# An attention and FFN kernel: the FFN's matmuls dealt between the attention steps of later batches

## What is computed

```python
# x (8, 256, 512): 8 batches, 256 channels, 512 positions; mask (8, 512)
Q, K, V = (proj(W) for W in (Wq, Wk, Wv))          # 16 heads of 16 channels
att = softmax((Q @ K.T / 4 + b) * m + (1 - m) * -1e30)
y = att @ V                                        # back to (8, 256, 512)
gate, up = y @ Wg.T, y @ Wu.T                      # 512 -> 4096, weights of 4-bit codes x scales per 32
gelu = tanh(0.7978845608 * (gate + 0.044715 * gate**3)) * gate * 0.5 + gate * 0.5
out = x + (gelu * up) @ Wd.T                       # 4096 -> 512
```

## Time and profile before

| | us |
|---|---|
| median of 3 runs (lowest to highest) | 1612.29 (1604.95 to 1619.18) |
| the profiled execution | 1610.11 |
| its span, first to last instruction | 1608.3 |
| busy in the span: PE / DVE / ACT / POOL | 1510.4 / 695.6 / 534.6 / 270.4 |
| mean granted clock of PE | 0.937 |
| moved by DMA | 63.04 MB, mean 39 GB/s |

### The profile page before, as it was taken

One profiled execution on the slowest core, in us unless ns is written; L12 is line 12 of the kernel. 1 busy time (PEld: TensorE's weight loads), 2 busy tenths in 40 slices (PEclk: granted clock), 3 DMA queues, 4 the chain that ended last, 5 costly groups with the idle time before them and its releaser, 6 DMA issues.

```text
span 1608.3 us, 19482 instructions
## 1 busy us (share of the span) xinstructions
PE 1510.4 (94%) x7376; PEld 597.7 (37%) x7376; DVE 695.6 (43%) x1113; ACT 534.6 (33%) x701; POOL 270.4 (17%) x146
## 2 busy tenths in 40 slices
PE   3989889898989889999999999999999999999999
PEld 1222222222322224444444444444444444444444
DVE  5858676776777562323323233323233232122122
ACT  1447464564656463222222222222222222111111
POOL 2012112121211212122112212211221221000000
PEclk7779896897898899999999999999999999999999
DMA  5112221212221103001001000100100010000000
GB/s 165 44 51 59 65 63 43 61 44 57 67 69 42 51 21 124 20 20 40 20 20 33 26 20 20 39 20 20 36 23 20 20 39 1 0 26 26 0 26 26
DMA packets 32662, 63.04 MB, mean 39 GB/s; under 512 B 5584, under 2 KB 14928, under 8 KB 32480
## 3 DMA queue, kind: packets, MB, share of 16 engines
q1 hardware_dynamic: 29760, 59.42, 12.5%
q10 hardware_dynamic: 2848, 2.90, 0.5%
HBM read 49.43 MB, written 12.61 MB: 39 GB/s over the span
## 4 chain that ended last, share of the span: by engine, by line
PE 82%; DMA 6%; DVE 5%; SPq 3%; ACT 2%; issue 1%; ACTq 1%; POOL 1%; POOLq 0%; DVEq 0%
PE psum L828 14%; PE psum L830 14%; PE psum L829 14%; PE psum L769 7%; PE psum L899 7%; PE psum L901 7%; PE psum L900 7%; PE psum L798 6%; DMA wide<-seed_rows 4%; DVE maxima L638 3%; PE psum L784 3%; PE psum L756 2%; PE psum L805 1%; PE psum L746 1%; DMA wide<-max_lo 1%
## 5 line engine op out<-in xcount | busy, mean ns | idle before, releaser
L638 DVE TENSOR_REDUCE maxima<-psum 128x1 f32<-128x512 f32 x512 | 332.3, 685 | 161.9 <-PE psum L769 158.3
L703 DVE SCALAR_TENSOR_TENSOR small<-psum,small 128x512 f32<-128x512 f32 x128 | 88.5, 691 | 592.6 <-issue 306.6
L544 ACT ACTIVATE big<-psum 128x1024 f32<-128x1024 f32 x256 | 253.4, 1024 | 214.8 <-PE psum L784 198.2
L769 PE MATMUL psum<-wide 51*128 51x512 f16 x512 | 211.3, 447 | 68.3 <-DMA wide<-seed_rows 51.1
L580 ACT ACTIVATE small<-psum 128x512 f32<-128x512 f32 x128 | 76.4, 597 | 421.1 <-PE psum L830 421.1
L334 POOL TENSOR_TENSOR dq_w<-dq_code,dq_scales 128x1536 f32<-128x1536 f16 x32 | 109.8, 3433 | 541.8 <-DVE dq_code L371 541.8
L590 ACT CAST in_hi<-small 128x512 f16<-128x512 f32 x128 | 79.1, 618 | 361.8 <-DVE small L703 361.8
L828 PE MATMUL psum<-y_hi,wide 128*128 x512 | 194.1, 379 | 2.6 <-POOL wide L346 2.6
L828 PE MATMUL psum<-y_hi,w_even_hi 128*128 (+1 forms) x512 | 194.2, 379 | 1.2 <-POOL w_even_lo L346 1.2
L829 PE MATMUL psum<-y_lo,w_even_hi 128*128 (+1 forms) x512 | 194.0, 379 | 0.0
L830 PE MATMUL psum<-y_hi,w_even_lo 128*128 (+1 forms) x512 | 194.0, 379 | 0.0
(11 more groups left out here) (83 smaller groups left out, 1366.2 us busy)
## 6 DMA issues: line engine op xcount, KB each, us to landing
dq_packed<-packed SPq DMA_DIRECT2D x32, 384.0 KB
dq_scales<-scales SPq DMA_DIRECT2D x32, 384.0 KB
wide<-qk_parts SPq DMA_DIRECT2D x64, 128.0 KB
qk_parts<-wide SPq DMA_DIRECT2D x60, 128.0 KB
small<-x SPq DMA_DIRECT2D x8, 512.0 KB, 4.1
wide<-qk_parts SPq DMA_DIRECT2D x64, 64.0 KB
big<-x SPq DMA_DIRECT2D x4, 1024.0 KB, 9.5
out<-big SPq DMA_DIRECT2D x16, 256.0 KB, 2.1
```

Of the source, the lines that this page charges most:

```text
L544: nc.scalar.activation(p_exp[:, k, :, i], p_score[:, 2 * i:2 * i + 2, :], ACT.Exp, scale=SCORE_SCALE).then_inc(exp_done, 1)
L638: nc.vector.reduce_max(maxima[:, g % 2, n:n + 1], p_max[:, n % 2, :], AX.X).then_inc(max_red, 1)
L769: nc.tensor.matmul(p_max[:, n % 2, :], q_stack[rows, side, s, t * P:(t + 1) * P], k_stack[rows, side, s, :], start=True, stop=True).then_i ...
```

## The change

The FFN now goes by chunks of two batches, all 32 units for one chunk, and chunk c is worked on while attention computes batches 2c+2 and 2c+3. One generator, `schedule()`, gives all engines one order. Batches 0 and 1 (`SOLO`) and the first steps of batch 2 run alone. Then each attention step that PE takes part in is followed by `len(rest) // left` FFN steps of the chunk. An FFN step is three matmuls: `G0` to `G3` gate, `U0` to `U3` up, `D` one of 16 down steps, which come after each fourth unit for the four units before. Chunk 3 runs after attention is over.

- Weights are decoded in chunk 0 (two units ahead; the first two in batches 0 and 1), used from a ring of 8 units (`w_ring`), stored in DRAM as fp16 halves (`spill_unit`, 0.79 MB) and reloaded in the later chunks three units ahead (`reload_unit`).
- PSUM in the mixed part: one pair of banks for scores (before: two), gate bank 2, up bank 3, the sums in 2 and 3 too (before: gate and up two banks each, sums four). In chunk 3 gate and up alternate again.
- Max tiles of batches 2 on are made in pairs, upper and lower rows, and one `reduce_pair` reads both banks. PE issues nothing at an even `m` and two tiles at an odd one.
- Gelu becomes `square` (ACT), `cubic` (DVE), `tanh` (ACT), `gelu_part` (DVE), `inter_part` (DVE); the remainder of the result moves from DVE to POOL (`inter_low`). One `inter` buffer in place of two; five slots of `in_hi` and `in_lo`.
- DVE adds to `acc` after every 4 units: 128 additions in all, before 64. `acc` holds one chunk; rows are loaded and stored by chunk.
- Decode has no separate sign and magnitude tiles; packed codes and scales have two slots. The loops of the FFN are unrolled.

```diff
-GROUPS = 4
-UNITS = F // P // GROUPS
+UNITS = F // P
+GROUP = 4
+RING = 2 * GROUP
+AHEAD_UNITS = 2
+LAST_CHUNK = (CHUNKS - 1) * UNITS
+LAST_SHARED = LAST_CHUNK // GROUP - 1
+SOLO = 2
...
+        def gate_bank(u):
+            return psum[:, 0 if u > LAST_CHUNK and u % 2 else 2, :]
+        def up_bank(u):
+            return psum[:, 1 if u > LAST_CHUNK and u % 2 else 3, :]
+        def out_bank(j, r):
+            return psum[:, 2 + r % 2 if j < LAST_SHARED else 4 + r, :]
...
+        def ffn(c):
+            for u in range(UNITS * c, UNITS * (c + 1)):
+                for step in ("G0", "G1", "G2", "G3", "U0", "U1", "U2", "U3"):
+                    yield u, step, None
+                if u >= GROUP and u % GROUP == 0:
+                    for r in range(4):
+                        for i in range(GROUP):
+                            yield u, "D", (u // GROUP - 1, r, i)
+            if c == CHUNKS - 1:
+                for step in ("G0", "G1"):
+                    yield STEPS, step, None
+                for r in range(4):
+                    for i in range(GROUP):
+                        yield STEPS, "D", (STEPS // GROUP - 1, r, i)
...
+        def schedule():
+            steps = list(attention())
+            ready = [n + 1 for n, (b, g, step, _) in enumerate(steps) if step == "YN" and g == 0 and b >= 2 and b % 2 == 0]
+            for b, g, step, arg in steps[:ready[0]]:
+                yield "attention", b, g, step, arg
+            for c in range(CHUNKS):
+                rest = list(ffn(c))
+                span = steps[ready[c]:ready[c + 1]] if c < CHUNKS - 1 else []
+                left = sum(on_pe(step) for _, _, step, _ in span)
+                for b, g, step, arg in span:
+                    yield "attention", b, g, step, arg
+                    if on_pe(step):
+                        count = len(rest) // left
+                        left -= 1
+                        for u, name, part in rest[:count]:
+                            yield "ffn", u, None, name, part
+                        rest = rest[count:]
+                for u, name, part in rest:
+                    yield "ffn", u, None, name, part
...
@@ scalar
+            for kind, b, g, step, arg in schedule():
+                if kind == "ffn":
+                    u = b
+                    if step == "G0" and u:
+                        inter_high(u - 1)
+                    elif step == "G1" and u + AHEAD_UNITS < UNITS:
+                        weight_scale(act, u + AHEAD_UNITS)
+                    elif step == "G2" and SOLO <= u + AHEAD_UNITS - 1 < UNITS:
+                        weight_hi(act, u + AHEAD_UNITS - 1)
+                    elif step == "G3":
+                        square(u)
+                    elif step == "U1":
+                        tanh(u)
+                    continue
...
@@ gpsimd
+                    if step == "G1" and u:
+                        inter_low(u - 1)
+                    elif step == "G3" and SOLO <= u + AHEAD_UNITS - 1 < UNITS:
+                        weight_lo(pool, u + AHEAD_UNITS - 1)
+                    elif step == "U2" and u + AHEAD_UNITS < UNITS:
+                        weight_f(pool, u + AHEAD_UNITS)
...
@@ vector
+            def reduce_pair(b, g, n):
+                dve.wait_ge(max_mm, 16 * q + n + 2)
+                nc.vector.reduce_max(maxima[:, g % 2, n // 2:n // 2 + 9:8], p_max, AX.X).then_inc(max_red, 2)
...
+            def cubic(u):
+                dve.wait_ge(square_s, u + 1)
+                nc.vector.scalar_tensor_tensor(out=gelu[:, u % 2, :], in0=gelu[:, u % 2, :], scalar=1.0,
+                                               in1=gate_bank(u), op0=ALU.add, op1=ALU.mult).then_inc(cubic_s, 1)
+            def gelu_part(u):
+                dve.wait_ge(tanh_s, u + 1)
+                nc.vector.scalar_tensor_tensor(out=gelu[:, u % 2, :], in0=gelu[:, u % 2, :], scalar=1.0,
+                                               in1=gate_bank(u), op0=ALU.add, op1=ALU.mult).then_inc(gelu_s, 1)
...
+            for kind, b, g, step, arg in schedule():
+                if kind == "ffn":
+                    u, n = b, b + AHEAD_UNITS
+                    if step == "G1" and n < UNITS:
+                        decode(dve, n, 0)
+                    elif step == "G2" and n < UNITS:
+                        decode(dve, n, 1)
+                    elif step == "G3" and n < UNITS:
+                        decode(dve, n, 2)
+                    elif step == "U0":
+                        cubic(u)
+                    elif step == "U1" and n < UNITS:
+                        decode(dve, n, 3)
+                    elif step == "U2":
+                        gelu_part(u)
+                    elif step == "U3":
+                        inter_part(u)
+                    elif step == "D" and arg[2] == GROUP - 1:
+                        add_rows(arg[0], arg[1])
...
@@ tensor
-                wait_from(pe, max_red, 16 * (4 * b + g) + n - 1)
-                e, i, t = n // 8, n // 4 % 2, n % 4
+                if b_now < SOLO or n % 2 == 0:
+                    wait_from(pe, max_red, 16 * (4 * b + g) + n - (1 if b_now < SOLO else 0))
+                e, i, t = n % 2, n // 8, n // 2 % 4
...
-                wait_from(pe, exp_done, n - 1)
+                wait_from(pe, exp_done, n - 1 if b < SOLO else n)
+                bank = 2 * i if b < SOLO else 0
...
+            def wait_bank(u, used, freed):
+                if u > LAST_CHUNK:
+                    wait_from(pe, freed, u - 1)
+                elif u > GROUP and u % GROUP == 1:
+                    pe.wait_ge(acc_add, 4 * (u // GROUP - 1) + used + 3)
+                else:
+                    wait_from(pe, freed, u)
...
@@ sync
+                    if step == "G0" and u < STEPS:
+                        if u + AHEAD_UNITS + 1 < UNITS:
+                            load_unit(sp, u + AHEAD_UNITS + 1)
+                        if UNITS <= u + AHEAD_UNITS + 1 < STEPS:
+                            reload_unit(sp, u + AHEAD_UNITS + 1)
+                    elif step == "U2" and u + AHEAD_UNITS - 1 < UNITS:
+                        if u == 0:
+                            spill_unit(sp, 0)
+                        spill_unit(sp, u + AHEAD_UNITS - 1)
```

More of the change, by code:

```diff
@@ L104, in build @@
             "p (e k o) -> p e k o", e=2, k=CK)[:, e] for e in range(2)] for i in range(3)]
-        gelu = small[:, 0:1024].rearrange("p (i t) -> p i t", i=2)
-        inter = small[:, 1024:2048].rearrange("p (i t) -> p i t", i=2)
+        gelu = sb("gelu", [P, 2, T], f32)
+        inter = sb("inter", [P, T], f32)
         av_sb = sb("av_sb", [P, T], f32)
@@ L186, in build @@
         acc_in = sem("acc_in")
+        w_out = [sem(f"w_out{i}") for i in range(RING)]
+        w_in = [sem(f"w_in{i}") for i in range(RING)]
         gate_mm = sem("gate_mm")
         up_mm = sem("up_mm")
+        square_s = sem("square_s")
+        cubic_s = sem("cubic_s")
+        tanh_s = sem("tanh_s")
         gelu_s = sem("gelu_s")
@@ L256, in head_of, with attention, on_pe @@
             return 8 * (g // 2) + 4 * e + 2 * (g % 2) + i
-        def batches(eng, body):
+        def attention():
             for b in range(B):
-                body(b, b % 2, b == 0, b == B - 1)
+                yield b, 0, "any", None
+                for g in range(QUADS):
+                    for step, arg in plan(g, b == 0, b == B - 1):
+                        yield b, g, step, arg
+            for step in ("A2", "A3", "AO", "Y", "YN"):
+                yield B, 0, step, None
+        def ffn(c):
[12 more added lines that the diff above has]
+                        yield STEPS, "D", (STEPS // GROUP - 1, r, i)
+        def on_pe(step):
+            return step[0] in "SmAY" and step not in ("AO", "YN") or step == "MT" or step[0:2] in WORK and step[2] in "ab"
+        def schedule():
[17 more added lines that the diff above has]
+                    yield "ffn", u, None, name, part
         def wait_from(eng, sem, value):
@@ L267, in wait_from @@
                 eng.wait_ge(sem, value)
-        def chunks(eng, body):
-            for g in range(GROUPS):
-                if g == 0:
-                    body(0, 0)
-                with eng.Fori(1 if g == 0 else 0, CHUNKS) as t:
-                    body(g, t)
         def wait_apart(eng, spare, sem, value):
@@ L597, in _, with square, tanh @@
-            chunks(act, chunk)
+            def square(u):
+                act.wait_ge(gate_mm, u + 1)
+                wait_from(act, inter_s, u - 1)
+                nc.scalar.activation(gelu[:, u % 2, :], gate_bank(u), ACT.Square,
+                                     scale=GELU_A ** 0.5 / (Y_SCALE * W_SCALE)).then_inc(square_s, 1)
+            def tanh(u):
+                act.wait_ge(cubic_s, u + 1)
+                nc.scalar.activation(gelu[:, u % 2, :], gelu[:, u % 2, :], ACT.Tanh,
+                                     scale=GELU_B / (Y_SCALE * W_SCALE)).then_inc(tanh_s, 1)
@@ L820, in _ @@
             for n in range(AHEAD):
```

(19 more changed lines are left out.)

530 lines of the change are left out of this document (253 added, 277 removed).

## The result

The changed kernel takes 1656.14 us (median of 4 runs, 1652.05 to 1662.40), the kernel before 1614.82 in runs beside it: a ratio of 1.0268, 95% interval 1.0207 to 1.0329. The prediction was 1574 in 1530 to 1650: the sign was wrong and the time lies above the range. Its profiled execution took 1662.4 us, its span is 1660.6; the sum that was forecast for that span is 1572.5, so 88 us are to be found. The profiled execution is the slowest of the four, 6 us above the median.

A forecast was written before the change was run, and what follows sets the result against it. It took attention's PE idling and half clock as the bound, the FFN having nothing left to gain. Solo 179, mixed work 1071, waits 36 + 20, chunk 3 266.5 made a span of 1572.5; with 1.5 more, 1574 us, range 1530 to 1650.

The forecast's parts named there:

- Solo: Batches 0 and 1 up to the first YN of batch 2, running alone: forecast to end at 179 us.
- that YN: First YN step of batch 2, end of the solo part: claimed reached at 175.4 us in the old kernel.
- the head's loads: Start of kernel: 0.8 MB more weights and 1 MB of x ahead of a stack transfer, 3.5 us, bounds 0 and 8.
- the forecast's own waits of 56: Mixed part: waits of 36 us in chunk 0 and 20 us in chunks 1 and 2, 10 each.
- decode steps on VectorE: Chunk 0, each unit: two steps of 0.95 and two of 0.55 us, 3.0 us together.
- The 36 us charged for waits: Chunk 0: stalls of 25 us in the two-F part, 9 with one F, plus POOL's other work; bounds 15 and 85.
- The loop of waits that the prediction walked: Chunk 0 decode: POOL's product, ScalarE's half, POOL's low half, then the next product, 8.2 us with hops, every unit.
- F: Mixed part: one FFN step of three matmuls on PE, 0.65 us; 1136 of them, 738 us.
- S: Mixed part, attention: two score matmuls on PE, 0.43 us; a pair of max tiles was given the same.
- rival 4: Mixed units: ScalarE changes its table between exp and tanh, two loads a unit, some 200 us, 1770; chance 0.02.
- Rival 2: Mixed part: the clock keeps falling; 1750 at mean clock 0.86, 1655 at 0.93; chance 0.09.
- Rival 1: Gate bank and decode step 0: chain and decode loop cost more than 92 us, 1648 in one case; chance 0.15.

The follow-up runs named there:

- the experiment: Changed kernel with the first FFN step of chunks 0, 1 and 2 moved six attention steps later: 1638.86 us, ratio 1.0102 to the kernel before.
- The even version: Changed kernel with that six-step later FFN start and weight decoding spread evenly, one unit every 12 FFN steps: 1590.88 us, ratio 0.9797 to the kernel before.
- the one with both sides cut: Changed kernel with POOL's two weight instructions and VectorE's four decode steps on 8 of 768 columns from the third unit on: 1568.57 us, one run.

## Why the prediction was wrong

**Solo, +35 us: a row misread.** "The old kernel is at that YN at 175.4 us" was false. The transposes `Y` of the kernel before, in order, lead to these two:

```profile
173.25 1.11 PE L805 MATMUL psum<-ident,av_sb 128*128 128x128 f32 x4
...
207.55 0.66 PE L805 MATMUL psum<-ident,av_sb 128*128 128x128 f32 x4
```

and in the changed kernel the first one of batch 2, and the first gate matmul behind it:

```profile
205.79 0.66 PE L907 MATMUL psum<-ident,av_sb 128*128 128x128 f32 x4
...
213.80 0.61 PE L930 MATMUL psum<-y_hi,w_ring 128*128 128x512 f16 x1 [5.90 <-POOL y_lo L525]
```

Batch 0 has three `Y` steps, since the first one of a batch belongs to the last quad of the batch before, and each later batch has four. So the one at 173.25, the sixth, is the third of batch 1; the eighth, at 207.55, is the first of batch 2, and the changed kernel reaches it 1.8 us earlier. So the head's loads cost nothing (3.5 were charged), and 34 us of attention that belong to the solo part were in no term: the mixed part was counted from the right step, the solo part ended at a wrong time. Cut rightly, attention after the solo part had this to give:

```profile
209.00:607.20 398.20, 354.65 (x1967) 100.16 (x1963) 271.88 (x469) 231.71 (x280) 72.77 (x64) 0.86 0.19 52
```

398 us against 333 of PE work at full clock, not 432. The sum without waits becomes 1551 of span, and waits have 57 us before the gain is gone, not 92. With the forecast's own waits of 56 the span would be 1607 against 1608.3: no change. This slip alone was the whole of the forecast gain.

**Chunk 0, +72: a price from rows in which nothing stood beside it.** The step that failed is "decode steps on VectorE (two of 0.95, two of 0.55 = 3.0)". In the kernel before POOL idled during them; beside POOL's products they take 5.73. The 36 us charged for waits became a loss of 108 (461.1 against 353 of work), where the bounds allowed 15 to 85: 77 of idle, and 31 of busy time beyond the forecast's work, at a granted clock of 0.92. The overlap was wrong: the sum let VectorE's steps and POOL's products run beside one another, and they don't. The loop of waits that the prediction walked exists, but taking its semaphore out gave 9 us; 63 of the 89 us appear only where both engines do their full work, and dealing the same work evenly gave back 52. With the right boundary and this loss alone the verdict "slower" follows: 1607 + 72 - 20 (chunks 1 and 2) is 1659.

**The wait for y_lo, not charged.** 14.8 us over the four chunks, and 17.6 by the experiment. The prediction looked for added waits in the FFN's chain and not at its first step.

**Right.** PE's own work in the mixed part: F at 0.65, S at 0.43, pairs at the price of S; chunk 1 took 367.5 against 363.6 of work, chunk 2 349.9 against 354. PE idles 5.9 and 6.9 us there, so the 10 us for each were too much. The paired reduce is 1.223 us (1.2), the inter remainder on POOL 1.17 (1.1), chunk 3 268.3 (266.5). PE waits for no stack transfer in the mixed part and for no reload. One table load in all:

```profile
L569 ACT ACT_TABLE_LOAD x1 | 1.3, 1283 | 11.6 <-PE psum L831 11.6
```

as the Trainium skill, "ScalarE: Activation LUTs", section "Table sets: the hidden batching unit", has it for exp and tanh. But the price of rival 4 was wrong by far: it put every load in the chain, 200 us, where 113 loads cost chunks 1 and 2 nothing.

**The clock.** In chunks 1 and 2 it is granted at 1.00, with one gate and one up bank in turn; in chunk 0, where PE idles 77 of 461 us, at 0.92, and at 0.98 with the waits cut away. So the fall follows the waits and adds to them (28 of the 89 us). Rival 2 happened in a mild form in chunk 0, through the waits and not beside them. The rule that the prediction weighed, of the Trainium skill, "TensorE: Matmul & The Clock Gate", section "A second HAM failure mode: psum-queue depth-cycling", is borne out in part: one gate and one up bank alone did not do it, since PE idled only 13 us in 717 and the clock held 1.00; where the decode made PE wait 70 us for the gelu that frees the gate bank, the clock fell to 0.92.

**Rival 1** is the nearest of the cases (waits over 92 us, 0.15): the losses over the forecast's work are 108 + 4 - 4 = 108 us. Its place was right, its cause only in part.

**What stays open.** The even version's chunk 0 still takes 29 us more than the one with both sides cut. Its decode steps take 4.76 us a unit, not 3.0, so part of it is the same meeting; how much, no run separates. Nor does a run part the ports from the semaphores between VectorE and POOL within the 63 us. Also not tried: POOL's products on another engine.

## What to carry to other kernels

A duration is a price only beside what ran on the other engines when it was measured: before moving VectorE work with its operands in SBUF next to GpSimd work, look whether the two ever overlapped in the trace, and if not, let them stand end to end in the sum. Work dealt between other work should be dealt by its own count, not hung on steps that leave 112 of 368 without any. And a stage boundary taken from a trace is checked by counting the instructions that define it, from the start.

## What the runs showed of the hardware

- VectorE's decode steps, with all operands in SBUF, stand until a running GpSimd `tensor_tensor` has ended: 2.55 us for eight columns, ending 0.03 us after it. Instructions with an operand in PSUM pass (0.67 and 1.21 us, unchanged). It holds the other way round too: a GpSimd piece of 0.54 us took 1.26 behind a decode step.
- GpSimd's product of 128x1536 takes 3.44 us whole and 8 x 0.59 = 4.7 us in pieces of 128x192, its subtraction, where it meets no decode step, 3.10 and 8 x 0.54 = 4.4: about 0.16 us more for each piece in both.
- Table loads of 1.283 us on ScalarE, nearly two a unit, were hidden in chunks 1 and 2, with ScalarE busy for 53 and 50% of the time.
